# Projecting four tiles at a time, with four consecutive tokens in one partition, at the end of an attention and mixture-of-experts kernel

## What is computed

```python
s = attn(xn)            # 16 heads, 12 samples per token and head, at positions within 8 of the token
g = silu(ffn(xn))       # 8 experts, the best 2 for each token, hidden size 512
out = x + s * g
```

```python
out = out.transpose(0, 2, 1, 3).reshape(b, q, d)
return out @ wo.T + bo
```

## Time and profile before

| | us |
|---|---|
| median of 3 executions (lowest, highest) | 1522.35 (1520.65, 1523.67) |
| the profiled execution | 1519.66 |
| its span, from first to last instruction | 1518.0 |
| TensorE (PE) busy | 1376.2 (91%) |
| VectorE (DVE) busy | 1291.5 (85%) |
| ScalarE (ACT) busy | 824.7 (54%) |
| GpSimd (POOL) busy | 759.8 (50%) |

### The profile page before, as it was taken

How to read it: one execution, slowest core, us unless ns; L and a number is a source line. 1 busy time by engine, 2 the same in 40 slices (tenths; PEclk the granted TensorE clock), 3 DMA queues, 4 the chain that set the end, 5 groups by cost and what they waited for, 6 DMA issues and landing times.

```text
span 1518.0 us, 35944 instructions
## 1 busy us (share of the span) xinstructions
PE 1376.2 (91%) x13751; PEld 1097.0 (72%) x13752; DVE 1291.5 (85%) x1544; ACT 824.7 (54%) x1889; POOL 759.8 (50%) x530
## 2 busy tenths in 40 slices
PE   5998889996399999999999999989999968788888
PEld 4864555555288888888888888878888846566666
DVE  7837645654599999999999999999999999989971
ACT  2547766665265545455554555444554536566565
POOL 1001577440367768687776767657676642211011
PEclk9998999997699999999999999999999987898999
DMA  7935566666856866767676766747576679999897
GB/s 224 347 133 98 126 170 173 171 168 160 272 148 162 250 175 190 237 155 226 165 231 164 215 194 176 223 113 219 154 232 177 169 168 222 255 195 246 232 246 153
DMA packets 203995, 293.52 MB, mean 193 GB/s; under 512 B 25346, under 2 KB 160774, under 8 KB 203636
## 3 DMA queue, kind: packets, MB, share of 16 engines
q0 software_dynamic: 64672, 146.57, 37.2%
q1 hardware_dynamic: 137731, 144.88, 33.9%
q10 hardware_dynamic: 1488, 0.80, 0.2%
HBM read 182.83 MB, written 117.73 MB: 198 GB/s over the span
## 4 chain that ended last, share of the span: by engine, by line
DVE 53%; issue 7%; PE 6%; DMA 6%; SPq 2%; ACT 0%; POOL 0%; DVEq 0%; POOLq 0%; ACTq 0%
DVE gslope L1676 12%; DVE parts L1672 12%; DVE parts L1632 8%; DVE expert_mem L1598 5%; DMA band<-band_rows 5%; DVE parts L1644 3%; PE pB L1503 2%; DVE parts L1648 2%; DVE parts L1651 2%; PE pA L1488 1%; DVE gslope L1729 1%; DVE wgt L1737 1%; DVE prob L1724 1%; PE pY L1513 1%; DVE score L1655 1%
## 5 line engine op out<-in xcount | busy, mean ns | idle before, releaser
L1196 POOL DMA_INDIRECT moe_rows<-expert_mem,token_of x142 | 326.1, 2296 | 83.7 <-issue 41.1
L1469 PE MATMUL pA<-xsT,expert_mem 128*128 128x256 f32 x1136 | 259.0, 381 | 12.7 <-ACT xsT L1299 10.3
L1475 PE MATMUL pY<-expert_mem 128*128 x1136 | 269.0, 391 | 0.0
L1177 POOL DMA_INDIRECT expert_mem<-xn_rows,token_of x142 | 207.1, 1459 | 100.8 <-issue 90.5
L1469 PE MATMUL pB<-xsT,expert_mem 128*128 128x256 f32 x1136 | 256.8, 379 | 0.0
L1469 PEld LDWEIGHTS pA<-xsT,expert_mem 128*128 128x128 f32 x1136 | 216.6, 191 | 44.2 <-issue 13.6
L1475 PEld LDWEIGHTS pY<-expert_mem 128*128 128x128 f32 x1136 | 213.5, 193 | 43.6 <-issue 16.5
L1469 PEld LDWEIGHTS pB<-xsT,expert_mem 128*128 128x128 f32 x1136 | 215.8, 190 | 29.3
L1676 DVE TENSOR_REDUCE gslope<-parts 128x256 f32<-128x3072 f32 x64 | 214.7, 3354 | 2.2
L1672 DVE SCALAR_TENSOR_TENSOR parts<-posw,prob 128x768 f32<-128x768 f32 x240 | 213.6, 951 | 1.0
L1318 ACT ACTIVATE expert_mem<-pA,b1sel 128x256 f32<-128x256 f32 x284 | 111.3, 474 | 152.9 <-DVE expert_mem L1598 68.8
(11 more groups left out here) (206 smaller groups left out, 2085.4 us busy)
## 6 DMA issues: line engine op xcount, KB each, us to landing
expert_mem<-in_w_l POOLq DMA_DIRECT2D x71, 1024.0 KB, 6.9
band<-band_rows SPq DMA_DIRECT2D x256, 96.0 KB, 5.2
S_rows<-stage SPq DMA_DIRECT2D x256, 94.0 KB
band_rows<-wgt SPq DMA_DIRECT2D x12, 1536.0 KB, 6.7
xn_rows<-stage SPq DMA_DIRECT2D x16, 512.0 KB, 5.5
v_rows<-stage SPq DMA_DIRECT2D x16, 512.0 KB, 4.3
moe_rows<-zeros POOLq DMA_DIRECT2D x4, 2048.0 KB
out<-in_x SPq DMA_DIRECT2D x16, 512.0 KB, 8.7
```

The lines of the kernel that those rows point to most:

```text
L1177: nc.gpsimd.indirect_dma_start(out=xs[:, u, s], out_offset=None, in_=dram["xn"], in_offset=bass.IndirectOffsetOnAxis(ap=keep["inv"][:, 2 * ...
L1196: nc.gpsimd.indirect_dma_start(out=dram["moe"], out_offset=bass.IndirectOffsetOnAxis(ap=keep["inv"][:, 2 * n + s:2 * n + s + 1], axis=0), ...
L1469: mm = nc.tensor.matmul(dst[:, c], w1[:, 1 - u, k, o * HID + c * P:o * HID + (c + 1) * P], xsT[:, k], start=(k == 0), stop=(k == KC - 1))
L1475: mm = nc.tensor.matmul(pY[:, s], hid[:, h, c, s * P:(s + 1) * P], w2[:, c, ds(e * D, D)], start=False, stop=(s == 1 and c == HC - 1))
```

## The change

The projection is made for a unit at a time, in two halves, while the next unit's tiles are worked on. `outT` holds a whole unit, and half h projects the tokens 4p+2h and 4p+2h+1, p from 0 to 127, by taking every fourth column of `outT` as weights. Partition p then holds the four consecutive tokens 4p to 4p+3, and `unit_rows` is written as `"(p a) c -> p a c"`: what a partition loads or stores of a unit is one stretch of 4 KB in DRAM. The last unit goes as before. The bias comes first, as one matmul of 512 columns for a half. ScalarE copies halves of 512 columns. The buffers for finished units go from 10 to 8, because `outT` now lies in memory of the expert weights. TensorE's loop body grows from four tiles to eight. The three tables move exponentials, preparations and units.

```diff
-ROW_SLOTS = 10
+ROW_SLOTS = 8
...
-END_EXPONENT_AT = (0, 14, 28, 42)
-END_PREPARE_AT = (6, 21)
+END_EXPONENT_AT = (0, 18, 36, 51)
+END_PREPARE_AT = (8, 26)
...
-UNITS_AT = ({}, {5: 1, 7: 1}, {1: 1, 3: 1, 5: 1, 7: 1}, {1: 1, 3: 1, 6: 1}, {4: 1, 6: 1})
+UNITS_AT = ({}, {7: 1}, {1: 1, 3: 1, 5: 1, 7: 1}, {1: 1, 3: 1, 5: 1, 7: 1}, {4: 1, 6: 1})
...
+        outT = pool_mem[:, W2_F + LATE_F:W2_F + W1_F].rearrange("p (u c n) -> p u c n", u=2, c=KC)
...
         def unit_rows(t, k):
-            return t[k * GTOK:(k + 1) * GTOK, :].rearrange("(a p) c -> p a c", p=P)
+            rows = t[k * GTOK:(k + 1) * GTOK, :]
+            return rows.rearrange("(p a) c -> p a c", a=GROUP) if k < LAST else rows.rearrange("(a p) c -> p a c", p=P)
...
-                nc.scalar.activation(proj[:, k % ROW_SLOTS, t % GROUP], pJ[t % 2], ACT.Identity).then_inc(pj_ready, 1)
+                if i >= ROW_SLOTS and h == 0:
+                    act.wait_ge(out_stored[i % ROW_SLOTS], 16 * (i // ROW_SLOTS))
+                nc.scalar.activation(proj[:, i % ROW_SLOTS, 2 * h:2 * h + 2], pJ[h][:], ACT.Identity).then_inc(pj_ready, 1)
...
-            def project(t, u):
+            def project(i, h, u):
+
+                pe.wait_ge(outT_ready, GROUP * i + GROUP)
+                if not (isinstance(i, int) and i == 0):
+                    pe.wait_ge(pj_ready, 2 * i + h - 1)
+                nc.tensor.matmul(pJ[h][:], ones3[:], bo[:, None, :].broadcast_to([NB, 2, D]), start=True, stop=False)
+                for s in range(2):
+                    for c in range(KC):
+                        mm = nc.tensor.matmul(pJ[h][:, s], outT[:, u, c].rearrange("p (q a) -> p a q", a=GROUP)[:, 2 * h + s],
+                                              wo[:, c], start=False, stop=(s == 1 and c == KC - 1))
+                mm.then_inc(pj_done, 1)
...
-                    if not (first and j == 0):
-                        project(t - 1, (j + 1) % 2)
+                    if not first and not last and j % 2 == 0:
+                        project(i - 1, j // 2, 1 - u)
+                    if last and j < 2:
+                        project(i - 1, j, 1 - u)
...
-                dve.wait_ge(pj_ready, (k + 1) * GROUP)
+                dve.wait_ge(pj_ready, 2 * k + 2)
```

More of the change, by code:

```diff
@@ L955, in mix_block @@
         LATE_F = 2 * SUBS * D
-        assert W2_F == MOE_SLOTS * UNIT_F and W1_F == 2 * LATE_F and LATE_F + HID_F + ACT_F + XS_F + YS_F >= ROW_SLOTS * UNIT_F
+        assert W2_F == MOE_SLOTS * UNIT_F and W1_F == 2 * LATE_F and HID_F + ACT_F + XS_F + YS_F >= ROW_SLOTS * UNIT_F
+        assert LATE_F == 2 * KC * GTOK
         pool_mem = sb("expert_mem", [P, MOE_F + ACT_F + XS_F + YS_F])
@@ L999, in mix_block @@
         v = sb("vk", [P, 2, SUBS, D])
-        outT = sb("outT", [P, 2, KC, P])
         rel = sb("rel", [P, 1])
@@ L1012, in mix_block @@
         pV = [pB[:, 2 * u] for u in range(2)]
-        pJ = [pY[:, 0], pO[:, 0]]
+        pJ = [pY, pO]
         w1_loaded = [sem(f"w1_loaded{u}") for u in range(2)]
@@ L1434, in _ @@
                 evacuate_y(n, n % 2, n // 2)
[L1435 to L1442, removed]
+            for t in range(TILES):
+                if t > 0 and t + 1 < TILES:
+                    evacuate_band(t + 1, 0)
+                    evacuate_band(t + 1, 1)
+                evacuate_out(t)
+                i, j = t // GROUP, t % GROUP
+                if i > 0 and i < LAST and j % 2 == 0:
+                    evacuate_unit(i - 1, j // 2)
+                if i == LAST and j < 2:
+                    evacuate_unit(i - 1, j)
+                if i == LAST and j >= 2:
+                    for k in range(t - 2 if j == 2 else t - 1, t if j == 2 else t + 1):
+                        evacuate_tile(k)
                 if t in END_EXPONENT_AT:
@@ L1565, in _, with four_tiles @@
             pe.wait_ge(ys_ready, SLOT_PAIRS)
-            def four_tiles(i, first=False, last=False):
+            def four_tiles(i, u, first=False, last=False):
                 for j in range(GROUP):
@@ L1573, in four_tiles @@
                     times_v(t, j, i)
-                    if not (first and j == 0):
-                        project(t - 1, (j + 1) % 2)
[L1577 to L1581, removed]
+                    if not first and not last and j % 2 == 0:
+                        project(i - 1, j // 2, 1 - u)
+                    if last and j < 2:
+                        project(i - 1, j, 1 - u)
+                    if last and j >= 2:
+                        for k in range(t - 2 if j == 2 else t - 1, t if j == 2 else t + 1):
+                            project_tile(k)
+            four_tiles(0, 0, first=True)
+            for i in range(1, 3):
+                four_tiles(i, i % 2)
+            with pe.Fori(1, TILES // GROUP // 2 - 1) as i:
+                for u in range(2):
+                    four_tiles(i * 2 + u + 1, 1 - u)
+            four_tiles(LAST, LAST % 2, last=True)
         @block.vector
```

37 lines of the change are left out of this document (22 added, 15 removed).

## The result

The changed kernel takes 1561.58 us (median of 4 executions, 1559.98 to 1566.13) against 1522.42 for the kernel before, measured beside it: a ratio of 1.0274, interval 1.025 to 1.0298. It is 39 us slower; 1512 was forecast, with 1543 as the upper end. The profiled execution has a span of 1558.7 us in place of 1518.0.

The account below looks back on a forecast made before the run. VectorE's chain and TensorE's tiles, waiting for weights, were taken to bound the last stage; tile 51 31.7 us sooner, last weights at 1469.1 plus 38.9 ended the span 10.0 shorter: 1522.3 - 10.0 = 1512.3 us, range 1504 to 1543.

Parts of the forecast that it names:

- rival (a): Last stage: step 15's exponentials come late, tile 51 after 1441, and the kernel is slower, 1528 to some 1545; chance 0.28.
- 31.7 of gains: Tiles up to 51: projection 9.2, DMA packets 13.9, exponentials moved 5.0, fewer slow stretches 3.6; tile 51 copied at 1431.3.
- with the engines at 0.97 the tiles wait less by as much: Unit stores: 4 KB packets at 218 ns save DMA time over nine units, so tiles wait 13.9 us less.
- 0.20 a tile, 9.2 us: TensorE's projection by halves of 2.14 us saves 0.80 a unit, 9.2 us over 46 tiles.
- the column choice costs nothing in this sum: TensorE's projection: loading every fourth column as weights is covered by the matmuls, so it adds 0 us.
- ScalarE's 5.0: Step 15's exponentials, blocking ScalarE behind tile 42, move behind tile 51 and cost the tiles nothing: 5.0 us gained.
- the 3.6 for slower stretches: TensorE: fewer waits mean two fewer slow-clock stretches after waits, at 1.8 us each, 3.6 us gained.
- Both are met narrowly: Exponentials of steps 13 and 14: tile 18 is done by 1323.5 and tile 36 by 1393, as VectorE needs.
- Sum 38.9: From step 15's last weights at 1469.1 to the span's end at 1508.0: store, load, last tiles and tail, 38.9 us.
- (b): Rival, last stage: unit stores no longer hold up tile loads, no stall is left, time 1506; chance 0.22.
- (c): Rival, TensorE's projection: loading every fourth column doubles and shows, 18 us over eleven units, time to 1530; chance 0.04.
- (d): Rival, TensorE's eight-tile loop body: jumps wait for code, 12 to 18 us, time 1525 to 1530; chance 0.02.

Follow-up runs that it names:

- the lead repaired: The early request put on a kernel; on the change in full, 1638.65 us, ratio 1.0097 to the kernel before.
- the early request: A tile's weights asked for after the transposes of the tile four before, values still waiting for its products; on the kernel before, 1612.89 us, ratio 0.9927.
- The order alone: Kernel before with SyncE's queue issuing a tile's weights ahead of its value rows: 1612.83 us, ratio 0.9949.
- the repaired kernel: The change with exponentials and preparations back at their old tiles, plus the early request: 1620.68 us, ratio 0.9971.
- the one with the old layout: The change with exponentials and preparations back, plus contiguous token columns and 1 KB rows as in the kernel before: 1541.85 us, ratio 1.0116.
- The even split: The change with exponentials and preparations back, each half projection split between even and odd tile: 1627.01 us, ratio 1.0034; with the early request 1618.29 us.
- tables back: The change with exponentials (0, 14, 28, 42) and preparations (6, 21) back at their old tiles, units' places kept: 1543.02 us, ratio 1.0138.
- the pairs: Kernel before with tile projections and their ScalarE copies done two behind each even tile, none behind odd ones: 1627.57 us, ratio 1.0051.

## Why the prediction was wrong

**What held.** Two chains meet at the exponentials and at tile 60, and each us by which the exponentials of step 15 are late passes whole to the last weights: they are ready 35.5 us after them, as forecast (1475.4 and 1510.9). To the end it passes only as far as the weights, and not the tiles, come last. With the lead repaired, 20.5 us of waits for exponentials (11.7 and 8.8, against 1.0 without the two tables) bring the last weights 19.7 us later, and the time is 18.0 longer by the medians (13.6 in the two traces). Without the early request the two tables moved the last weights by 39.7 us (1471.2 to 1510.9) and the time by 18.6, since the tiles were late by themselves. The sign named in advance for rival (a) is the one that the trace shows: a wait of over 10 us at the exponentials of step 15 (23.2).

**Where the error lies in the sum.** The span was to end at 1508.0 and ended at 1558.7, 50.7 us later. Of these, 41.8 are tile 51, copied at 1473.1 in place of 1431.3: 31.7 of gains that did not come and 10.1 of loss. The other 8.9 are the way from the last weights to the end.

**The step that failed: "with the engines at 0.97 the tiles wait less by as much".** 13.9 us were booked as fewer bytes' time in the DMA engines. But what the tiles waited for was not the sum of the bytes. They waited because a load is asked for late, and behind others. The order alone is worth 8.1 us at equal bytes; in the repaired kernel the engines have a share of 0.98, as high as before, and the tiles hardly wait. A busy share near one was read as a bound, where the waits of the earlier trace rows said only "this load came late".

**The size in that step was wrong too.** Packets of a unit's store, from 1294 to 1296 in the changed kernel:

```profile
q0 software_dynamic: 83, 0.34, 88.5%
```

0.885 x 32 / 83 is 341 ns, near the 357 from which rival (a) was to decide, and not 218. Four times 102 is 408, so most of the surcharge goes with the bytes. The figure is rough, since two us hold a part of one store only. A store takes 128 x 341 / 16 = 2.7 us, not 1.7, in place of 3.3. With nine stores that is 5 us of engine time instead of 13.9. No run shows it to be worth anything: the one with the old layout, which gives up the strided columns as well, is no slower.

**TensorE's "0.20 a tile, 9.2 us".** The repaired round gives 0.10 a tile. The half of 2.14 is what contiguous columns would have cost (0.31 for the bias, 1.83 for the records), and "the column choice costs nothing in this sum" was wrong: with every fourth column the records take 2.09, so a half is 2.40, which takes back 0.13 of the 0.20 a tile. The greater error is of kind: the sum of TensorE's work was counted, not its distribution. The half projections are 0.2 us cheaper per pair, but they leave the odd tiles 6.6 us in which to load, where a load took 9.7. That is what ate the tiles' gain. The even split takes back 14.5 of 20.6 us, the earlier request all of it (both across batches). In the trace of the even split, which is its fastest execution, the tiles are as quick as before, 270.3 us from tile 0 to tile 63 against 271.5; 2.8 of its remaining 6.1 us lie behind the last transfer, as told below. The prediction had listed each edit's cost and hidden work, and never asked what else the projection was covering: the way of a load.

**ScalarE's 5.0 and the 3.6 for slower stretches.** The block at tile 42 did go, but tile 42 was at 1429.6 by then, later than before. The slow stretches did not get fewer: the clock stays at 0.87 in the stretch shown, and with tables back it is 0.85.

**"Both are met narrowly".** They weren't, for three reasons that are each in the rows. VectorE wants the exponentials of steps 13 and 14 before it writes the next scores (L1691), not where it sums them: it stood from 1319.9 and 1399.3. The first two places of the earlier trace rows, moved by as much as the weights of the step before had moved (-2.5 and +6.6), are 1324.7 and 1403.3, so it wants them 4 to 5 us sooner than I had them wanted. From the copy of tile 18 to the exponentials' end it is 4.5 us, not 2.3: the copy of a half projection, which the change itself put there, waits 1.65 us and takes 0.60. And the tile was there 6.2 us after the 1323.5 that it had to meet.

**"Sum 38.9".** From the last weights to the end it was 47.8. The weights of tile 60 took 3.5 us from the landing of the store to the issue of the last of their four transfers, where 1.4 were booked. From the first transposes behind that load to its last matmul TensorE took 21.1 and not 18.0: it started at the lower clock (1.94 for the transposes of tile 60), and the values of tile 59 were still to be done. And from there to the end it was 10.0 and not 6.9. The store and the load themselves took 6.4 and 5.8, near the 6.7 and 5.2 booked.

**The rivals.** (a) had the right place, sign and signs to look for, at 0.28, but gave at most some 1545: it priced lost gains only, and the tiles did not merely gain nothing, they got slower. (b) was wrong. (c) is true of the load and not of the time. The Trainium skill, "SBUF — State Buffer", in the note on SBUF "cachelines", says that crossing to a new line of 16 bytes at each access costs; here the load of such weights took 332 ns against 190, so the trace agrees. The matmuls covered all but 31 ns a record: not the doubling that this rival asked for, but not the nothing of the sum either. (d) did not happen. The Trainium skill, "Runtime: NRT & Kernel Launch", section on instruction fetch mechanics, warns of a stall at jumps outside two pages; the queues of the changed kernel from 1335 to 1530, four rounds of the body of eight tiles, are

```profile
q1 hardware_dynamic: 23913, 23.18, 48.3%
q0 software_dynamic: 3952, 16.12, 33.5%
q14 instruction: 7, 0.06, 0.1%
```

and instruction queue q8, which has 59 packets on the whole page, has none there. So the stall that the section warns of does not show in these rounds. That q8 is TensorE's own is inferred: its count went from 52 to 59 with the longer body.

**Where the expected gain is.** With the lead repaired, the tables back and the projection per unit (1620.68), the change is 7.8 us behind the kernel before with the same repair (1612.89). Their last weights come at the same distance from tile 0, 225.5 and 226.3 us. So it lies in the end: from the last weights to the end of the span 53.9 and 46.0 us. Of the 7.9 between them, 1.4 lie ahead of tile 60, with a load that TensorE waits 2.3 us for and a half at the lower clock behind it (3.73). The stretch from the copy of tile 60 to that of tile 63 has 3.5 (12.7 and 9.2), since two halves of unit 14 are still to be done there and not one tile. The last 3.0 lie behind the copy of tile 63, and 2.8 of these behind the last transfer of the whole kernel, where the views show no work at all: 5.9 us from its end to the end of the span against 3.1. The change in full has 5.8 there and the kernel before 3.0, so it is a fixed cost of the changed program. What it is, no run tells; these parts were read from the traces and not tried one by one.

**What stays open.** Why the pairs cost the kernel before only 6.6 us (9.5 by its trace) when the halves cost the change 20.6: 2.8 are the fixed cost at the end, and the lead is 6.8 instead of 6.6 us, but how often a short lead fails was not worked out, and the two were measured in different batches. The eight buffers and the places of the units were never put back, so their part is not known; with the lead repaired they, the wide copies and all the rest of the change come to no more than 7.8 us. Whether a table between the two (exponentials one or two tiles later than before) would gain with the lead repaired wasn't tried.

## What to carry to other kernels

An operation on a busy engine may be the cover of a load; before moving or bunching it, write down for each load the time from its request to its need, for every parity of the loop, and compare the smallest with the time that a load takes, not the mean. A DMA share near one does not show that bytes are the bound: exchange the order of two transfers, or ask for one earlier, and see. And work that one engine does for another at a place fixed by a third one's progress should stand as early as its input allows, since it is late by whatever that third one is late.

## What the runs showed of the hardware

- An accumulating packet of 4 KB took 341 ns where one of 1 KB took 102: the surcharge goes with the bytes for the most part.
- Weights read with a step of four floats load in 332 ns and contiguous ones in 190; eight matmuls of 256 columns in a row take 2.08 us in place of 1.83 with them, 31 ns each.
- A wait costs more than itself. After an idle of 3.21 us TensorE's transposes and half projection run at the lower of the two clocks, 1.2 GHz: 1.94 in place of 1.08 us and 3.73 in place of 2.18. The 2.4 us lost come on top of the wait. With the waits gone the granted clock of the stretch rises from 0.85 to 0.91. The change with tables back:

```profile
1456.20 1.94 PE L1503 MATMUL pA<-ident,band 128*96 128x128 f32 x8 [3.21 <-DMA band<-band_rows]
1458.07 1.23 PE L1518 MATMUL pB<-bandT,vk 96*32 96x32 f32 x64
1459.23 0.60 PE L1528 MATMUL pY<-bo,ones 3*128 3x512 bf16 x1
```

The granted clock of the 8 us before that idle time and of the 7 us behind it, in the last column but two:

```profile
1445.00:1453.00 8.00, 7.99 (x219) 7.01 (x217) 7.93 (x7) 6.88 (x13) 1.44 (x2) 1.00 0.67 151
1456.00:1463.00 7.00, 6.80 (x81) 5.29 (x82) 6.93 (x5) 1.81 (x4) 0.91 (x2) 0.50 0.83 197
```

- The kernel before took 99 and 103 us longer in two of the three batches (the second on the chip of the first, the third on another), and the traces have this ahead of the last stage; no run tells why. No kernel was traced in two batches, so that the last stage kept its length is likely and not shown: VectorE's step 15, from weights to weights, has 38.4 us both in the kernel before (first batch) and in the change with tables back and the early request (third).
